# Expert results added up in DRAM by the scatters, in two sums that blocks use in turn

## The chip, the cores and the metric

The kernel runs on one core of a Trainium2 chip. The metric is the time of one execution on the device, in microseconds, lower is better; a kernel's time is the median over its runs. Engines are called as in the profile: PE (TensorE; PEld are its weight loads), DVE (VectorE), ACT (ScalarE), POOL (GpSimd), and SP, which here only issues DMAs. "SPq", "ACTq" and "POOLq" are their queues.

## What is computed

One decoder layer on x of 16 sequences of 256 tokens with 256 features (4096 tokens in all), in f32. Three steps, each followed by a sum with its input and a layer norm:

```python
x = layernorm(x + attention(x))                  # one head, its own weighting function before the softmax
x = layernorm(x + cross_attention(x, ctx, ctx))  # 16 heads, in chunks of 64 positions
x = layernorm(x + ffn(x))
# ffn: 32 experts of width 128, each token goes to 4 of them, plus one shared expert of width 256
mixed  = (sel * topk_w[:, :, None]).sum(1)       # sel: the 4 chosen experts' outputs of a token
shared = (silu(h @ sg.T) * (h @ su.T)) @ sd.T
ffn    = mixed + shared
```

The change concerns the last step: how the four expert results of a token, its shared part and its residual come together before the last layer norm.

## The kernel before

**Phase 1, one sequence after the other.** A software pipeline over t in range(nseq + 5) runs attention, cross attention, the router and the shared expert of several sequences at once. Each engine has its own hand-written order of steps, guarded by semaphores; the queue of SP is one such order: `load_xT`, `load_x`, `load_c`, `store_acc`, `load_rest`. `load_rest(i)` fills the DRAM table `routed` with zeros once (at i == 0) and loads a sixteenth of the expert weights for each i. `vec_acc` forms residual + shared expert for two tokens per partition and `store_acc` writes them to the DRAM tensor `base` (4096 rows of 1 KB). POOL scatters each token's row four times into `routed`, into the regions of its experts (`pool_scattera`, `pool_scatterb`), with the gate weight and the destination row in two more columns.

**Phase 2, blocks of 128 rows.** The rows of one expert form blocks; there are 160 blocks, handled in turns of 8 (`UNROLL`). For each block SP loads 128 rows into one of 16 buffers `rowsb` (L1494), PE transposes them (`pe_xbT`, L277), multiplies with the gate and up weights (`pe_gu`, L583), transposes the hidden block, multiplies with the down weights (`pe_down`, L596); ACT scales the result by the gate weight into one of four buffers `yb` (`act_yb`, L924) once the scatter of four blocks before has landed; DVE computes the destination rows `idcol` (`vec_idx`, L1246), where rows beyond a block's end go to rows that nobody reads; POOL scatters `yb` into the DRAM tensor `y` (L1419). `y` has a row of its own for each of the 4 choices of each token, 16384 rows, so no two scatters touch the same row and none waits for another. Behind the row load of block 16, SP issues one load of the whole of `base` into `base_sb` (L1497).

**Phase 3, the end.** SP waits until all scatters have landed. Then 16 groups (`GROUPS`) of two tokens per partition (`FT` = 2): SP loads the four rows of each token into one of 8 buffers `f4` (`STEPS`, L611), from group 8 on only once the store of eight groups before has landed. POOL adds rows 2 and 3 (L652) and `base_sb` (L655); DVE adds rows 0 and 1 (L620), then POOL's sum (L622), takes `bn_stats` and `bn_aggr` (L626, L629), adds epsilon (L631); POOL takes the power -0.5 (L661), one group late; DVE makes the bias (L636), ACT normalizes (L674) and stores (L678).

Of the kernel before, what the change touches and what calls it, by code (L numbers as in the profile page):

```python
# [5 lines left out]
P = 128  # L6
D = 256
DK = D // P
S = 256
T = S // P  # L10
# [13 lines left out]
ROWS = 16  # L24
YS = 4
FT = 2
STEPS = 8
# [6 lines left out]
    "a_tanh", "a_v", "a_vo", "a_x1", "a_x1T", "a_x2", "a_x2T", "a_xbT", "a_yb", "a_z", "g_frs", "g_iota", "g_own",  # L34
    "g_pow1", "g_pow2", "g_row", "g_rs1", "g_rs2", "g_sum", "g_xc", "g_xc2", "ld_base", "ld_cT", "ld_const", "ld_w",
    "ld_we", "ld_x", "ld_xT", "p_av1", "p_av2", "p_den", "p_down", "p_gu", "p_hbT", "p_k", "p_out2", "p_pTa",
    "p_pTb", "p_prT", "p_q", "p_rank", "p_router", "p_s1", "p_s2", "p_setup", "p_sg", "p_shout", "p_spread", "p_su",
    "p_tab", "p_v", "p_vo", "p_x1T", "p_x2T", "p_xbT", "p_z", "st_base", "st_rowa", "st_rowb", "st_zrow", "v_acc",
    "v_const", "v_fve", "v_h1", "v_hb", "v_hb1", "v_hbT", "v_hs", "v_idx", "v_idx1", "v_key", "v_msel", "v_mx",
    "v_mxa", "v_mxb", "v_nblk", "v_nmr", "v_o", "v_onehot", "v_own", "v_r", "v_rden", "v_rep", "v_route", "v_setup",  # L40
    "v_sha", "v_shb", "v_sum", "v_tab", "v_ve1", "v_ve2", "v_zrow",
# [12 lines left out]
def constants(nseq):  # L54
# [15 lines left out]
        n * TOPK + np.arange(blocks)[None, :] * P + p[:, None],  # L70
# [8 lines left out]
def build(nc, d, out):  # L79
# [9 lines left out]
    y = nc.dram_tensor("y", (TOPK * N + BLOCKS * P, D), F32).ap()  # L89
    base = nc.dram_tensor("base", (N, D), F32).ap()  # L90

    ctx = ExitStack()
    with ctx:
        def sb(name, shape, dt=F32):
            return ctx.enter_context(nc.sbuf_tensor(f"{name}_tile", shape, dt))
# [134 lines left out]
        base_sb = sb("base_sb", [P, TILES, D])  # L230
        f4 = [w_flat[:, u * TOPK * FT * D:(u + 1) * TOPK * FT * D].rearrange("p (k t d) -> p k t d", k=TOPK, t=FT)
# [370 lines left out]
        def flat(a):  # L602
            return a.rearrange("p t d -> p (t d)")

        def sync_out(e):
            for a in range(YS):
                e.wait_ge(SEM[f"st_y{a}"], 16 * BLOCKS // YS)
            for g in range(GROUPS):
                u = g % STEPS
                after(e, SEM[f"st_out{u}"], 16 * (g // STEPS))  # L610
                e.dma_start(f4[u][:, :, :, :],  # L611
                            y[0:TOPK * N, :].rearrange("(k p j) d -> p k j d", k=TOPK, p=P)
                            [:, :, g * FT:(g + 1) * FT, :]).then_inc(SEM[f"ld_f{u}"], 16)

        def vec_out(e, ch):

            def sums(g):
                u, n = g % STEPS, g // STEPS + 1
                e.wait_ge(SEM[f"ld_f{u}"], 16 * n)
                ch(e.tensor_tensor(flat(f4[u][:, 0, :, :]), flat(f4[u][:, 0, :, :]), flat(f4[u][:, 1, :, :]), ALU.add))  # L620
                e.wait_ge(SEM["g_sum"], g + 1)
                e.tensor_tensor(flat(f4[u][:, 0, :, :]), flat(f4[u][:, 0, :, :]), flat(f4[u][:, 2, :, :]), ALU.add)\  # L622
                    .then_inc(SEM["v_sum"], 1)
                e.wait_ge(SEM["v_sum"], g + 1)
                for t in range(FT):
                    m = e.bn_stats(fst[u][:, t, :], f4[u][:, 0, t, :])  # L626
                ch(m)
                for t in range(FT):
                    m = e.bn_aggr(fag[u][:, t, :], fst[u][:, t, :])  # L629
                ch(m)  # L630
                e.tensor_scalar(fve[u][:, :], fag[u][:, :, 1], LN_EPS, None, ALU.add).then_inc(SEM["v_fve"], 1)  # L631
# [13 lines left out]
        def pool_out(e):  # L645

            def sums(g):
                u, n = g % STEPS, g // STEPS + 1
                if g == 0:
                    e.wait_ge(SEM["ld_base"], 16)  # L650
                e.wait_ge(SEM[f"ld_f{u}"], 16 * n)
                e.tensor_tensor(flat(f4[u][:, 2, :, :]), flat(f4[u][:, 2, :, :]), flat(f4[u][:, 3, :, :]), ALU.add)\  # L652
                    .then_inc(SEM["g_own"], 1)
                e.wait_ge(SEM["g_own"], g + 1)
                e.tensor_tensor(flat(f4[u][:, 2, :, :]), flat(f4[u][:, 2, :, :]),  # L655
                                flat(base_sb[:, g * FT:(g + 1) * FT, :]), ALU.add).then_inc(SEM["g_sum"], 1)
# [740 lines left out]
        def _(e):  # L1397
            e.iota(dest_id[:, :, :], [[N, TOPK], [1, T]], base=-T, channel_multiplier=TILES).then_inc(SEM["g_iota"], 1)
            e.wait_ge(SEM["v_setup"], 1)
            e.wait_ge(SEM["v_const"], 1)  # L1400
            for t in range(nseq + 5):
# [12 lines left out]
                if live(t - 3):  # L1414
                    pool_row(e, t - 3)
            for n in range(BLOCKS):
                e.wait_ge(SEM["a_yb"], n + 1)
                e.wait_ge(SEM["v_idx"], n + 1)
                e.indirect_dma_start(y, bass.IndirectOffsetOnAxis(ap=idcol[n % ROWS][:, :], axis=0), yb[n % YS][:, :],  # L1419
                                     None).then_inc(SEM[f"st_y{n % YS}"], 16)  # L1420
# [4 lines left out]
        def _(e):  # L1425
# [32 lines left out]
            def load_rest(e, i):  # L1458

                if i == 0:  # L1460
# [4 lines left out]
                        .then_inc(SEM["st_zrow"], 16)  # L1465
                share = E // nseq * 3 * D
# [22 lines left out]
            for n in range(BLOCKS):  # L1489
# [5 lines left out]
                if n == ROWS:  # L1495
                    e.wait_ge(SEM["st_base"], 16 * nseq)
                    e.dma_start(base_sb[:, :, :], base.rearrange("(p j) d -> p j d", p=P)).then_inc(SEM["ld_base"], 16)  # L1497
# [51 lines left out]
```

## Time and profile before

| | us |
|---|---|
| median of 3 runs | 902.51 (901.99 to 903.1) |
| the profiled execution: its time | 904.18 |
| its span in the profile | 902.4 |
| first scatter to y / last scatter to y, start | 559.9 / 827.9 |
| first load of the end, start | 830.4 |

| engine | busy us | share of the span |
|---|---|---|
| PE | 761.9 | 84% |
| DVE | 581.8 | 64% |
| ACT | 464.1 | 51% |
| POOL | 451.5 | 50% |

The shares are averages over three phases with different limits: phase 1 ends at about 548 us, phase 2 at 830, phase 3 at 902. Within each, the windows and the timeline tell more than the page's totals. A POOL row for a scatter covers the issuing of the DMA, not its landing; the landing is a separate figure.

### The profile page before, as it was taken

What the parts mean: (1) busy time and instruction counts of PE and PEld (TensorE: products, weight loads), DVE (VectorE), ACT (ScalarE), POOL (GpSimd) and SP (SyncE); (2) the same over time, 40 slices, a digit from 0 to 9 for tenths busy, and PEclk for the clock granted to TensorE, in tenths of its full rate; (3) what the DMA queues carried; (4) which work ended last, traced back from release to release, by engine and by line L of the source; (5) the groups of instructions that cost most, each with busy time, mean ns of one, the idle gap of its engine ahead of it and who ended that gap; (6) DMA issues with size and microseconds to landing.
All of it is one profiled execution on the core that took longest, in us unless ns stands there. A gap on an engine that the chain in (4) does not pass through costs nothing.

```text
span 902.4 us, 24334 instructions
## 1 busy us (share of the span) xinstructions
PE 761.9 (84%) x7772; PEld 640.7 (71%) x7772; DVE 581.8 (64%) x2337; ACT 464.1 (51%) x1185; POOL 451.5 (50%) x533
## 2 busy tenths in 40 slices
PE   4678899999999999999999566899999999995000
PEld 3457788888888888888887444688888888884000
DVE  1233488888888788888888764454555545552897
ACT  0335665656656566566664102466666666663122
POOL 0011115545555454654645662455555555554997
PEclk9779999999999999999999866999999999998555
DMA  5083113323243232433331123955455555443994
GB/s 215 23 189 130 49 53 126 118 93 96 104 136 116 93 105 98 136 102 102 98 132 62 61 99 107 321 171 165 151 166 158 157 164 158 156 147 110 392 337 162
DMA packets 68909, 125.39 MB, mean 139 GB/s; under 512 B 9649, under 2 KB 42417, under 8 KB 68402
## 3 DMA queue, kind: packets, MB, share of 16 engines
q1 hardware_dynamic: 50610, 81.74, 29.8%
q0 software_dynamic: 13824, 37.90, 11.2%
q10 hardware_dynamic: 4352, 4.20, 1.3%
q8 instruction: 67, 1.10, 0.5%
q14 instruction: 56, 0.46, 0.2%
HBM read 73.30 MB, written 50.50 MB: 137 GB/s over the span
## 4 chain that ended last, share of the span: by engine, by line
PE 78%; DVE 10%; issue 3%; DMA 3%; POOL 2%; ACT 2%; SPq 0%; ACTq 0%; POOLq 0%; DVEq 0%
PE bank L583 14%; PE bank L277 11%; PE bank L596 7%; PE bank L392 4%; PE bank L353 3%; PE bank L313 3%; PE bank L540 3%; PE bank L380 3%; PE bank L334 3%; PE bank L370 3%; PE bank L325 3%; PE bank L486 3%; PE bank L528 3%; DVE w_expert_tile L620 3%; PE bank L517 3%
## 5 line engine op out<-in xcount | busy, mean ns | idle before, releaser
L1419 POOL DMA_INDIRECT y<-yb_tile,idcol_tile x160 | 153.4, 959 | 131.3 <-ACT yb_tile L924 129.0
L583 PE MATMUL bank<-w_expert_tile,xbT_tile 128*128 x640 | 168.8, 387 | 4.1 <-ACT xbT_tile L759 4.1
L1253 DVE COPY hbT_tile<-bank 128x128 f32<-128x128 f32 x160 | 46.6, 292 | 123.6 <-PE bank L277 123.6
L583 PEld LDWEIGHTS bank<-w_expert_tile,xbT_tile 128*128 128x128 f32 x640 | 110.4, 192 | 16.5 <-issue 7.8
L1386 POOL DMA_INDIRECT routed<-row_tile,idx_tile x64 | 63.0, 985 | 86.6 <-PE bank L409 67.1
L924 ACT ACTIVATE yb_tile<-bank,rowsb_tile 128x256 f32<-128x256 f32 x160 | 75.7, 473 | 47.9 <-PE bank L596 41.8
L596 PE MATMUL bank<-w_expert_tile,hbT_tile 128*128 x320 | 95.8, 381 | 0.0
L1354 POOL TENSOR_TENSOR rs_tile<-ve_tile,half_neg_tile 128x2 f32<-128x2 f32 x16 | 11.4, 715 | 157.2 <-DVE ve_tile L1023 157.2
L918 ACT ACTIVATE gb_tile<-bank 128x128 f32<-128x128 f32 x160 | 44.4, 278 | 61.7 <-PE bank L583 61.7
L1393 POOL DMA_INDIRECT routed<-row_tile,idx_tile x64 | 65.7, 1027 | 17.7 <-issue 17.7
L759 ACT ACTIVATE xbT_tile<-bank 128x256 f32<-128x256 f32 x160 | 60.1, 376 | 26.3 <-PE bank L277 25.9
L277 PE MATMUL bank<-const_tile,rowsb_tile 128*128 128x128 f32 x320 | 62.7, 278 | 2.7 <-DMA rowsb_tile<-routed 2.5
L277 PEld LDWEIGHTS bank<-const_tile,rowsb_tile 128*128 128x128 f32 x320 | 43.9, 143 | 23.2 <-issue 6.1
L596 PEld LDWEIGHTS bank<-w_expert_tile,hbT_tile 128*128 128x128 f32 x320 | 48.3, 191 | 12.6 <-issue 0.6
L1236 DVE SCALAR_TENSOR_TENSOR hb_tile<-gb_tile,bank 128x128 f32<-128x128 f32 x160 | 44.8, 280 | 8.9 <-ACT gb_tile L918 8.8
L1240 DVE TENSOR_TENSOR hb_tile<-hb_tile,bank 128x128 f32<-128x128 f32 x160 | 45.9, 287 | 5.6
L674 ACT ACTIVATE w_expert_tile<-w_expert_tile,fnmr_tile,frs_tile 128x256 f32<-128x256 f32 x32 | 17.5, 593 | 56.2 <-DVE fnmr_tile L636 55.7
L277 PE MATMUL bank<-const_tile,hb_tile 128*128 128x128 f32 x160 | 43.6, 273 | 0.0
L1370 POOL COPY row_tile<-x_tile 128x512 f32<-128x512 f32 x64 | 37.0, 619 | 5.3 <-DMA routed<-row_tile,idx_tile 5.3
L1348 POOL TENSOR_TENSOR xc_tile<-x_sb_tile,c_out_tile 128x256 f32<-128x256 f32 x32 | 23.0, 740 | 30.7 <-DVE c_out_tile L1286 26.9
L540 PE MATMUL bank<-w_shared_out_tile,hs_tile 128*128 128x256 f32 x128 | 34.7, 419 | 0.3 <-DVE hs_tile L1161 0.3
L313 PE MATMUL bank<-xT_tile,g_qk_tile 128*128 128x256 f32 x128 | 33.1, 405 | 2.2 <-DVE c_out_tile L1286 2.2
(206 smaller groups left out, 1863.1 us busy)
## 6 DMA issues: line engine op xcount, KB each, us to landing
rowsb_tile<-routed SPq DMA_DIRECT2D x160, 129.0 KB, 2.2
w_expert_tile<-y SPq DMA_DIRECT2D x16, 1024.0 KB, 8.8
w_expert_tile<-w_expert SPq DMA_DIRECT2D x16, 768.0 KB, 6.3
cT_tile<-ctxT SPq DMA_DIRECT2D x16, 384.0 KB, 3.5
routed<-zrow_tile SPq DMA_DIRECT2D x1, 4128.0 KB, 22.5
xT_tile<-xT SPq DMA_DIRECT2D x16, 256.0 KB, 3.3
x_sb_tile<-x SPq DMA_DIRECT2D x16, 256.0 KB, 3.6
base<-acc_sb_tile SPq DMA_DIRECT2D x16, 256.0 KB
```

What stands on the lines that cost most here:

```text
L277: return e.transpose(o, i, ident)
L313: m = e.matmul(bank[1][:, db * S:(db + 1) * S], g_qk[:, k, db * P:(db + 1) * P], xT[:, k, :], start=k == 0, stop=k == DK - 1)
L540: m = e.matmul(bank[0][:, t * D:(t + 1) * D], hs[:, k, t * P:(t + 1) * P], w_shared_out[:, k, :], start=k == 0, stop=k == DK - 1)
L583: m = e.matmul(bank[2 + u % 2][:, 0:2 * EI], xbT[u % 2][:, k * P:(k + 1) * P], w_flat[:, bass.ds(w * 3 * D + k * D, D)], start=k == 0, sto ...
L596: e.matmul(bank[6 + u % 2][:, 0:D], hbT[u % 2][:, :], w_flat[:, bass.ds(w * 3 * D + 2 * D, D)], start=True, stop=True).then_inc(SEM["p_dow ...
L759: e.activation(o, i, ACT.Copy).then_inc(SEM[done], 1)
L924: e.activation(yb[n % YS][:, :], bank[6 + u % 2][:, 0:D], ACT.Copy, scale=rowsb[n % ROWS][:, D:D + 1])\
L1240: e.tensor_tensor(hb[u % 2][:, :], hb1[u % 2][:, :], bank[2 + u % 2][:, EI:2 * EI], ALU.mult)\
L1253: e.tensor_copy(hbT[u % 2][:, :], bank[4 + u % 2][:, 0:EI]).then_inc(SEM["v_hbT"], 1)
L1386: e.indirect_dma_start(routed, bass.IndirectOffsetOnAxis(ap=idx[:, 0, k:k + 1], axis=0), row[:, k, 0, :], None).then_inc(SEM["st_rowa"], 16)
L1393: e.indirect_dma_start(routed, bass.IndirectOffsetOnAxis(ap=idx[:, 1, k:k + 1], axis=0), row[:, k, 1, :], None).then_inc(SEM["st_rowb"], 16)
L1419: e.indirect_dma_start(y, bass.IndirectOffsetOnAxis(ap=idcol[n % ROWS][:, :], axis=0), yb[n % YS][:, :], None).then_inc(SEM[f"st_y{n % YS} ...
```

## The change

The four rows per token in `y` give way to two sums, `y[0]` and `y[1]`, of one row per token each (plus 128 rows that nobody reads). The scatter of block n adds into `y[n % 2]` (`compute_op=ALU.add`). Since blocks of different experts can hold the same token, the scatter of block n waits until that of block n - 2 has landed. `base` is now the first 4096 rows of `y[0]`, so residual and shared part are in the sum from the start; `y[1]` and the unread rows of `y[0]` are filled with zeros by two stores that SP issues at i == 2 of phase 1. POOL waits for all base stores and both fills before its first scatter. The load of `base` is gone. The end loads two rows per token in place of four, has 16 buffers in place of 8, and adds the two rows: POOL for the second token of each partition, DVE for the first.

```diff
-STEPS = 8
+SUMS = 2
+STEPS = 16
...
-        n * TOPK + np.arange(blocks)[None, :] * P + p[:, None],
+        np.tile(n + p[:, None], (1, blocks)),
...
-    y = nc.dram_tensor("y", (TOPK * N + BLOCKS * P, D), F32).ap()
-    base = nc.dram_tensor("base", (N, D), F32).ap()
+    y = [nc.dram_tensor(f"y{u}", (N + P, D), F32).ap() for u in range(SUMS)]
+    base = y[0][0:N, :]
...
-        base_sb = sb("base_sb", [P, TILES, D])
...
-                e.dma_start(f4[u][:, :, :, :],
-                            y[0:TOPK * N, :].rearrange("(k p j) d -> p k j d", k=TOPK, p=P)
-                            [:, :, g * FT:(g + 1) * FT, :]).then_inc(SEM[f"ld_f{u}"], 16)
+                for k in range(SUMS):
+                    e.dma_start(f4[u][:, k, :, :],
+                                y[k][0:N, :].rearrange("(p j) d -> p j d", p=P)[:, g * FT:(g + 1) * FT, :])\
+                        .then_inc(SEM[f"ld_f{u}"], 16)
...
-                e.wait_ge(SEM[f"ld_f{u}"], 16 * n)
-                ch(e.tensor_tensor(flat(f4[u][:, 0, :, :]), flat(f4[u][:, 0, :, :]), flat(f4[u][:, 1, :, :]), ALU.add))
+                e.wait_ge(SEM[f"ld_f{u}"], 16 * SUMS * n)
+                ch(e.tensor_tensor(f4[u][:, 0, 0, :], f4[u][:, 0, 0, :], f4[u][:, 1, 0, :], ALU.add))
+                e.bn_stats(fst[u][:, 0, :], f4[u][:, 0, 0, :])
                 e.wait_ge(SEM["g_sum"], g + 1)
-                e.tensor_tensor(flat(f4[u][:, 0, :, :]), flat(f4[u][:, 0, :, :]), flat(f4[u][:, 2, :, :]), ALU.add)\
-                    .then_inc(SEM["v_sum"], 1)
-                e.wait_ge(SEM["v_sum"], g + 1)
-                for t in range(FT):
-                    m = e.bn_stats(fst[u][:, t, :], f4[u][:, 0, t, :])
-                ch(m)
+                ch(e.bn_stats(fst[u][:, 1, :], f4[u][:, 0, 1, :]))
...
-                if g == 0:
-                    e.wait_ge(SEM["ld_base"], 16)
-                e.wait_ge(SEM[f"ld_f{u}"], 16 * n)
-                e.tensor_tensor(flat(f4[u][:, 2, :, :]), flat(f4[u][:, 2, :, :]), flat(f4[u][:, 3, :, :]), ALU.add)\
-                    .then_inc(SEM["g_own"], 1)
-                e.wait_ge(SEM["g_own"], g + 1)
-                e.tensor_tensor(flat(f4[u][:, 2, :, :]), flat(f4[u][:, 2, :, :]),
-                                flat(base_sb[:, g * FT:(g + 1) * FT, :]), ALU.add).then_inc(SEM["g_sum"], 1)
+                e.wait_ge(SEM[f"ld_f{u}"], 16 * SUMS * n)
+                e.tensor_tensor(f4[u][:, 0, 1, :], f4[u][:, 0, 1, :], f4[u][:, 1, 1, :], ALU.add)\
+                    .then_inc(SEM["g_sum"], 1)
...
-            e.iota(dest_id[:, :, :], [[N, TOPK], [1, T]], base=-T, channel_multiplier=TILES).then_inc(SEM["g_iota"], 1)
+            e.iota(dest_id[:, :, :], [[0, TOPK], [1, T]], base=-T, channel_multiplier=TILES).then_inc(SEM["g_iota"], 1)
...
+            e.wait_ge(SEM["st_base"], 16 * nseq)
+            e.wait_ge(SEM["st_zero"], 16 * 2)
             for n in range(BLOCKS):
+                e.wait_ge(SEM["v_idx"], n + 1)
+                if n >= SUMS:
+                    e.wait_ge(SEM[f"st_y{(n - SUMS) % YS}"], 16 * ((n - SUMS) // YS + 1))
                 e.wait_ge(SEM["a_yb"], n + 1)
-                e.wait_ge(SEM["v_idx"], n + 1)
-                e.indirect_dma_start(y, bass.IndirectOffsetOnAxis(ap=idcol[n % ROWS][:, :], axis=0), yb[n % YS][:, :],
-                                     None).then_inc(SEM[f"st_y{n % YS}"], 16)
+                e.indirect_dma_start(y[n % SUMS], bass.IndirectOffsetOnAxis(ap=idcol[n % ROWS][:, :], axis=0),
+                                     yb[n % YS][:, :], None, compute_op=ALU.add).then_inc(SEM[f"st_y{n % YS}"], 16)
...
+                if i == 2:
+                    e.dma_start(y[1].rearrange("(j p) d -> p j d", p=P),
+                                zrow[:, 0:D].rearrange("p (j d) -> p j d", j=1).to_broadcast([P, N // P + 1, D]))\
+                        .then_inc(SEM["st_zero"], 16)
+                    e.dma_start(y[0][N:N + P, :], zrow[:, 0:D]).then_inc(SEM["st_zero"], 16)
...
-                if n == ROWS:
-                    e.wait_ge(SEM["st_base"], 16 * nseq)
-                    e.dma_start(base_sb[:, :, :], base.rearrange("(p j) d -> p j d", p=P)).then_inc(SEM["ld_base"], 16)
```

## Rows read from the trace of the kernel before

**Rows 1.** Windows: PE, PEld, DVE, ACT, POOL busy, clock, DMA share, GB/s

```profile
...
566.00:583.00 17.00, 12.93 (x69) 10.31 (x68) 6.17 (x29) 7.31 (x24) 6.92 (x8) 1.00 0.96 360
585.00:827.00 242.00, 240.33 (x1294) 196.41 (x1292) 121.52 (x578) 148.38 (x432) 139.53 (x147) 1.00 0.50 155
840.00:896.00 56.00, 0.00 (x0) 0.00 (x0) 53.90 (x121) 15.30 (x28) 54.13 (x45) 0.50 0.88 311
```

**Rows 2.** Timeline of POOL, expert stretch: start, length, instruction, idle before

```profile
...
559.90 0.96 POOL L1419 DMA_INDIRECT y<-yb_tile,idcol_tile  x1 [15.67 <-ACT yb_tile L924]
...
571.29 0.96 POOL L1419 DMA_INDIRECT y<-yb_tile,idcol_tile  x1 [0.67 <-ACT yb_tile L924]
...
585.86 0.96 POOL L1419 DMA_INDIRECT y<-yb_tile,idcol_tile  x1 [0.67 <-ACT yb_tile L924]
...
602.48 0.96 POOL L1419 DMA_INDIRECT y<-yb_tile,idcol_tile  x1 [0.67 <-ACT yb_tile L924]
604.40 0.96 POOL L1419 DMA_INDIRECT y<-yb_tile,idcol_tile  x1 [0.96 <-ACT yb_tile L924]
```

**Rows 3.** Timeline of the end, the first sum, one group, the last power

```profile
...
835.83 0.69 DVE L620 TENSOR_TENSOR w_expert_tile<-w_expert_tile 128x512 f32<-128x512 f32 x1 [11.30 <-DMA w_expert_tile<-y]
...
882.00 1.76 DVE L620 TENSOR_TENSOR w_expert_tile<-w_expert_tile 128x512 f32<-128x512 f32 x1
...
883.18 1.14 POOL L661 TENSOR_TENSOR frs_tile<-fve_tile,fhalf_tile 128x2 f32<-128x2 f32 x1
...
883.80 0.69 DVE L622 TENSOR_TENSOR w_expert_tile<-w_expert_tile 128x512 f32<-128x512 f32 x1
884.29 1.32 POOL L652 TENSOR_TENSOR w_expert_tile<-w_expert_tile 128x512 f32<-128x512 f32 x1
...
885.69 1.27 POOL L655 TENSOR_TENSOR w_expert_tile<-w_expert_tile,base_sb_tile 128x512 f32<-128x512 f32 x1
885.74 1.76 DVE L620 TENSOR_TENSOR w_expert_tile<-w_expert_tile 128x512 f32<-128x512 f32 x1
...
897.06 0.69 POOL L661 TENSOR_TENSOR frs_tile<-fve_tile,fhalf_tile 128x2 f32<-128x2 f32 x1 [1.52 <-DVE fve_tile L631]
```

**Rows 4.** Page, group of POOL's 128x256 sums: busy us, mean ns

```profile
...
L1348 POOL TENSOR_TENSOR xc_tile<-x_sb_tile,c_out_tile 128x256 f32<-128x256 f32 x32 | 23.0, 740 | 30.7 <-DVE c_out_tile L1286 26.9
```

**Rows 5.** Timeline, the last scatter and the first load of the end

```profile
...
827.92 0.96 POOL L1419 DMA_INDIRECT y<-yb_tile,idcol_tile  x1 [0.30 <-issue]
830.36 50.03 SPq L611 DMA_DIRECT2D w_expert_tile<-y  x16
```

**Rows 6.** DMA issues of the whole run: count, KB each, median us to landing

```profile
...
rowsb_tile<-routed SPq DMA_DIRECT2D x160, 129.0 KB, 2.2
...
routed<-zrow_tile SPq DMA_DIRECT2D x1, 4128.0 KB, 22.5
...
base_sb_tile<-base SPq DMA_DIRECT2D x1, 4096.0 KB, 13.9
```

**Rows 7.** Timeline of SP's queue around the two places of a fill

```profile
...
50.01 10.74 SPq L1467 DMA_DIRECT2D w_expert_tile<-w_expert  x1
...
109.70 1.40 SPq L1467 DMA_DIRECT2D w_expert_tile<-w_expert  x1
121.31 0.33 SPq L1438 DMA_DIRECT2D xT_tile<-xT  x1
```

**Rows 8.** DMA issues from 49 to 72 us, the load behind the fill

```profile
...
w_expert_tile<-w_expert SPq DMA_DIRECT2D x1, 768.0 KB, 23.9
```

**Rows 9.** Timeline of PE, first use of the xT in question

```profile
...
143.12 1.89 PE L313 MATMUL bank<-xT_tile,g_qk_tile 128*128 128x256 f32 x8
```

**Rows 10.** All scatters to y: us from issue to landing

```profile
...
DMA to landing us min/median/max: 2.4/2.5/11.0
```

**Rows 11.** DMA queues from 585 to 827 us: packets, MB, share of 16 engines

```profile
...
q1 hardware_dynamic: 19518, 17.90, 28.9%
q0 software_dynamic: 7018, 19.19, 20.3%
```

More of the change, by code:

```diff
@@ L33 @@
     "a_gb", "a_hg", "a_k", "a_norm", "a_num", "a_pTa", "a_pTb", "a_pr", "a_prT", "a_q", "a_sc", "a_sha", "a_shb",
[L34 to L38, printed above, removed]
+    "a_tanh", "a_v", "a_vo", "a_x1", "a_x1T", "a_x2", "a_x2T", "a_xbT", "a_yb", "a_z", "g_frs", "g_iota", "g_pow1",
+    "g_pow2", "g_row", "g_rs1", "g_rs2", "g_sum", "g_xc", "g_xc2", "ld_cT", "ld_const", "ld_w", "ld_we", "ld_x",
+    "ld_xT", "p_av1", "p_av2", "p_den", "p_down", "p_gu", "p_hbT", "p_k", "p_out2", "p_pTa", "p_pTb", "p_prT",
+    "p_q", "p_rank", "p_router", "p_s1", "p_s2", "p_setup", "p_sg", "p_shout", "p_spread", "p_su", "p_tab", "p_v",
+    "p_vo", "p_x1T", "p_x2T", "p_xbT", "p_z", "st_base", "st_rowa", "st_rowb", "st_zero", "st_zrow", "v_acc",
     "v_const", "v_fve", "v_h1", "v_hb", "v_hb1", "v_hbT", "v_hs", "v_idx", "v_idx1", "v_key", "v_msel", "v_mx",
     "v_mxa", "v_mxb", "v_nblk", "v_nmr", "v_o", "v_onehot", "v_own", "v_r", "v_rden", "v_rep", "v_route", "v_setup",
-    "v_sha", "v_shb", "v_sum", "v_tab", "v_ve1", "v_ve2", "v_zrow",
+    "v_sha", "v_shb", "v_tab", "v_ve1", "v_ve2", "v_zrow",
     *(f"{n}{u}" for n in ("ld_f", "st_out") for u in range(STEPS)),
@@ L228, in build @@
         yb = [sb(f"yb{u}", [P, D]) for u in range(YS)]
-        base_sb = sb("base_sb", [P, TILES, D])
-        f4 = [w_flat[:, u * TOPK * FT * D:(u + 1) * TOPK * FT * D].rearrange("p (k t d) -> p k t d", k=TOPK, t=FT)
+        f4 = [w_flat[:, u * SUMS * FT * D:(u + 1) * SUMS * FT * D].rearrange("p (k t d) -> p k t d", k=SUMS, t=FT)
               for u in range(STEPS)]
```

## The prediction

> **What bounds the kernel now.** I read the table of windows first, to split the run into what is different: the expert stretch from 560 to 828 us and the end from 830 to 902 us. In the expert stretch TensorE is busy for 240.33 of 242 us at a granted clock of 1.00, POOL for 139.53, and the DMA engines half of the time [rows 1]. So there TensorE sets the pace, and everything else has room. The timeline of POOL gives that pace: scatters start at 559.90 and 571.29 with seven steps between them, 1.627 us each, and one step in eight is 1.92 (602.48 to 604.40), the turn's own cost; a turn of eight blocks takes 7 x 1.627 + 1.92 = 13.3 us [rows 2]. POOL issues for 0.96 us and sleeps for 0.67 until ACT has written yb [rows 2].
>
> At the end TensorE does nothing. Between 840 and 896 POOL is busy for 54.13 of 56 us and DVE for 53.90 [rows 1]. The timeline of one group there (882.00 to 885.74, 3.74 us) shows POOL without a gap: L661 1.14, L652 1.32, L655 1.27, together 3.73 [rows 3]. DVE's L620 takes 1.76 where L622, the same shape, takes 0.69 [rows 3]: it sits beside POOL's operations, so DVE's full look is partly waiting. POOL's three operations bound the end, and the DMA engines, 0.88 busy at 311 GB/s [rows 1], are close behind.
>
> **The end, step by step.** Each of the 16 groups moves 1.05 MB in and 0.26 MB out now; after, 0.52 MB in and 0.26 out, 12.6 MB in all against 21. At full business the two DMA-heavy stretches give 311/0.88 = 353 and 360/0.96 = 375 GB/s [rows 1], so 12.6 MB take 33.5 to 35.6 us, 2.1 to 2.2 us per group. POOL keeps one sum of 128x256 (0.74 by L1348, the same kind and shape [rows 4]) and the power (0.69 alone, 1.14 beside DVE [rows 3]): 1.4 to 1.9 us. DVE loses L620 (1.76), has half of L622 (about 0.36, up to 0.9 if it is stretched in the ratio of L620 to L622), and keeps the statistics and small operations, 3.74 - 1.76 - 0.69 = 1.3: 1.7 to 2.2 us. Three engines near 2 us; the largest is the DMA, and I take 2.15. The sixteen buffers in place of eight take away the loads' wait for stores, so nothing else holds the loads back.
>
> The first sum started 5.5 us after the first load's issue (830.36 to 835.83 [rows 3, 5]); with half the bytes (0.52 MB less at 360 GB/s is 1.5 us) it starts after about 4. Then fifteen groups of 2.15, then the last group: 1.9 on DVE and, as now from the last power's start to the end of the span, 902.4 - 897.06 = 5.3 us [rows 3]. That is 830.4 + 4 + 32.2 + 7.2 = 873.8, against 902.4: 28.6 us saved. The bounds: with 1.8 us per group 34, with 2.5 us 23.
>
> **The base load.** base_sb, 4.1 MB with 13.9 us to landing [rows 6], is issued among the row loads and does collide: from 571.29 to 585.86 six steps take 14.57 us where 6 x 1.627 = 9.8 would do [rows 2], in the stretch where the DMA engines are 0.96 busy [rows 1]. It goes away whole: 4.8 us saved.
>
> **The zero fill.** A new store of 4.3 MB is put into SP's queue at i == 2, like the fill of routed at i == 0, which took 22.5 us to land [rows 6] and whose follower, a weight load at 50.01, held SP's issue for 10.74 us [rows 7] and landed after 23.9 [rows 8]. The new one comes at about 109.7; the weight load behind it then issues until about 121, when SP turns to the next xT anyway (121.31) [rows 7]. What is late is the xT and x of the next sequence. By the first fill the weight load is in 24 us after the fill's issue, here at 134, and xT and x, 0.26 MB each behind it, by about 136; TensorE wants xT at 143.12 [rows 9]. Seven microseconds of cover, so zero. Were the loads later than that, TensorE would wait once for what overruns 143.12: a fill of twice the length, 45 us, would cost 15. The second fill (0.13 MB) and POOL's waits for the last base store lie long before the first scatter at 559.90; both cost nothing. POOL's iota only changes its pattern.
>
> **The scatters: the unknown.** POOL must now see scatter n - 2 landed before it issues n, and each scatter also adds. Behind the wait on POOL stands every later scatter; ACT waits for them by the four yb buffers, then TensorE through the banks. So a pair of blocks costs at least L + r, L from issue to landing, r from the landing to the next issue. TensorE's own pace gives 13.3 / 4 = 3.33 us per pair. The plain scatter has L = 2.4 to 2.5 [rows 5, 10]. For r, POOL's gap between issues with nothing to wait for is 0.30 [rows 5], and I take 0.25. So the plain scatter would need 2.7 of 3.33: the turn-taking alone is free, and adding may cost L another 0.6 before it shows (L = 3.08). Beyond that each 0.1 us of L costs 80 pairs x 0.1 = 8 us. The gain of 33 us is gone at L = 3.5.
>
> No row shows an adding DMA. The lower bound is that of the plain one, 2.4. The upper bound, a read that is done before the write begins: a row load from DRAM, 2.2 us [rows 6], and then the scatter, 2.4, or 4.6. Between them: the scatters' queue takes 20.3% of 242 us on the DMA engines for 147 scatters, 0.33 us each [rows 11]. If each row is read as well, and rows are pipelined, that is another 0.33 us, and a DRAM access ahead of the first. A row load's engine time is 28.9% of 242 us over 134, 0.52 us [rows 11]; of its 2.2 us the other 1.7 are issue, access and landing, and I give the access 0.3, because SP's issue alone takes 0.33 at least [rows 7] and the landing is a way of its own. That makes L = 3.1. It is nearer to the pipelined end since a scatter's 128 rows are independent, eight for each engine. Then: 80 x 0.02 and some irregular landings, about 2 us, and 0.6 for the last landing. DMA engines then are some two thirds busy, not full. Were the issue on POOL longer too, it would bind by itself from 13.3 / 8 - 0.30 = 1.36 us; 0.96 now.
>
> What the rows show is a scatter whose 0.33 us of engine time is a small part of its 2.4 us [rows 10, 11]. The Trainium skill, page Collectives: The Full Stack, section on the bandwidth ceiling, says that a reduction in the DMA engine is slower because it needs two source reads, not for the addition. By that rule alone L would be about 2.8 and the stretch would stay free; my sum has 3.1.
>
> **The sum**, against the profiled execution's 904.2 us: -28.6 (end) - 4.8 (base) + 0 (fill) + 2.6 (scatters) = -31, so 873; that execution is 1.7 above the median of 902.5, so 872.
>
> **The rivals.** (1) The same mechanism, with an adding scatter of 3.2 to 3.45 us: part of the gain is paid back on the pairs, 880 to 899 us. For it: 0.1 to 0.4 us over my L is nothing beside a price that no row shows. Against: the engine time doubled explains only 0.33.
> (2) The other side: L above 3.5. POOL's wait for st_y of n - 2 replaces ACT's yb as what ends its idle time, TensorE starves, and the kernel is slower. At L = 4.0 a pair takes 4.25, 74 us more than 3.33 over 80 pairs, 943 us; at the bound of 4.6, 122 us more, 991 us. For it: landing is latency, not bytes, and an adding scatter has two latencies in a row. Against: pipelining. In that bound the read is 2.2 us; the Trainium skill, DMA: Bandwidth & Descriptors, section on latency, has 0.2 us on average and 2 us at high load for an HBM access, so by its second figure this rival would win; the trace has no row for it. The engines here are half busy [rows 1].
> (3) Making descriptors for an addition doubles POOL's issue: 1.92 + 0.30 = 2.22 per block against 1.66, 90 us more, some 959 us. Nothing in the rows speaks for a doubling; the routed scatters cost the same issue with other rows.
> (4) The end is held by something else (DVE and POOL taking turns on every group, 2.5 us per group): 878.
>
> **The numbers.** My forecast, L at most 3.2 with the end as worked out, has 0.46 and, alone, the range 864 to 881. Rival 4 has 0.05, rival 1 has 0.14. Rival 2 has 0.29 (0.16 of it up to 945), rival 3 has 0.04. About 0.02 is left where gain and loss cancel. So faster by over 0.2% 0.65, within 0.2% (1.8 us, about what a measurement of this kernel can tell from no change) 0.02, slower 0.33. The range for 8 in 10 goes from 864 to 945, leaving out the longest landings and the doubled issue.
>
> **What would show it.** Right: POOL's idle time before the scatters still ended by ACT's yb; scatters' landing below 3.1; steps of 1.63 without the hole at 571; TensorE busy over 0.95 in the stretch; the end about 43 us long with 2.1 to 2.2 us from group to group; the sequence after the fill no longer than the others. Wrong: POOL waiting for the y landings, granted clock and TensorE's share falling between 560 and 828, an issue above 1.36 us.

## The result: slower by 9.6%

The changed kernel takes 989.34 us (median of 4 runs, 986.5 to 989.91) where the kernel before takes 902.25 beside it. The ratio is 1.096, 95% interval 1.0935 to 1.0984. The forecast was 872 us, in a range of 864 to 945. The profiled execution took 986.5 us, its span is 984.7.

The windows give the same columns as [rows 1]: busy PE, PEld, DVE, ACT, POOL, clock, DMA share, GB/s.

```profile
585.00:827.00 242.00, 179.34 (x890) 137.45 (x888) 90.32 (x395) 91.45 (x294) 153.46 (x99) 0.99 0.66 108
...
950.00:980.00 30.00, 0.00 (x0) 0.00 (x0) 26.98 (x110) 15.89 (x30) 24.95 (x32) 0.50 1.00 366
```

TensorE is busy for 179 of 242 us in the expert stretch, against 240 [rows 1]; its granted clock is still at the upper level of 2.4 GHz (0.99), so the clock has no part in the loss. At the end the DMA engines are now full. POOL's timeline shows the stretch (the answer to [rows 2]):

```profile
588.83 1.56 POOL L1415 DMA_INDIRECT y<-yb_tile,idcol_tile  x1 [1.30 <-ACT yb_tile L916]
590.69 1.56 POOL L1415 DMA_INDIRECT y<-yb_tile,idcol_tile  x1 [0.30 <-issue]
593.80 1.56 POOL L1415 DMA_INDIRECT y<-yb_tile,idcol_tile  x1 [1.54 <-ACT yb_tile L916]
595.66 1.56 POOL L1415 DMA_INDIRECT y<-yb_tile,idcol_tile  x1 [0.30 <-issue]
598.69 1.56 POOL L1415 DMA_INDIRECT y<-yb_tile,idcol_tile  x1 [1.47 <-ACT yb_tile L916]
```

Two things are new. The issue takes 1.56 us in place of 0.96. And the scatters come in pairs, 4.97 and 4.89 us from pair to pair, where TensorE's pace is 3.33. The releaser in these rows misleads: ACT's yb named here is not the one that POOL scatters next. ACT's own row says what it starts on:

```profile
593.16 0.47 ACT L916 ACTIVATE yb_tile<-bank,rowsb_tile 128x256 f32<-128x256 f32 x1 [2.43 <-DMA y<-yb_tile,idcol_tile]
```

ACT waits for the landing of the scatter issued at 588.83, because its buffer of four comes free with it, and POOL's scatter of 593.80 waits for that same landing, because it adds into the same sum; its own yb had been written from 588.19 on. The trace's record of that landing has 593.08, 4.25 us after the issue. Both were asleep on this one event: ACT starts 0.08 us after it and POOL 0.72 us after it, and 4.25 + 0.72 is the pair's 4.97. POOL starts 0.64 us after ACT, and since ACT's write of 0.47 us has ended just before, the profile puts POOL's idle time down to ACT. The waits of ACT from 585 to 927 us (us in total, times, longest) and the chain of the page tell the cause plainly:

```profile
ACT yb_tile L916 <- DMA y<-yb_tile,idcol_tile: 196.3, 133, 3.6
```

```profile
PE 47%; DMA 41%; DVE 6%; issue 2%; ACT 2%; POOL 1%; SPq 1%; ACTq 0%; POOLq 0%; DVEq 0%
DMA y<-yb_tile,idcol_tile 39%; PE bank L277 5%; PE bank L392 3%; PE bank L353 3%; PE bank L380 3%; PE bank L313 3%; PE bank L540 3%; PE bank L334 3%; PE bank L370 3%; PE bank L325 3%; PE bank L486 3%; PE bank L528 2%; PE bank L517 2%; PE bank L409 2%; PE bank L463 2%
```

39% of the span is the landing of scatters; the chain before had 3% of DMA in all. The landing itself (answer to [rows 10]) and the queues from 585 to 927 us (answer to [rows 11]; packets, MB, share of the 16 engines):

```profile
DMA to landing us min/median/max: 3.7/3.9/5.5
```

```profile
q0 software_dynamic: 20092, 18.31, 44.6%
q1 hardware_dynamic: 19219, 17.63, 20.8%
```

141 scatters take 44.6% of 342 us, 1.08 us of every DMA engine for one, where it was 0.33. The bytes of one scatter are the same, 0.13 MB, in three times the packets: 20092 for 141 scatters against 7018 for 147. The packet records give the sizes: an adding scatter has 128 packets of 1024 bytes and 16 of 4, a plain one 32 of 4096 and 16 of 4. A packet takes 0.12 us on average here and 0.11 before, so the larger number of packets is nearly the whole increase.

The end, in its timeline (answer to [rows 3] and [rows 5]):

```profile
942.03 1.56 POOL L1415 DMA_INDIRECT y<-yb_tile,idcol_tile  x1 [0.83 <-issue]
945.90 17.34 SPq L612 DMA_DIRECT2D w_expert_tile<-y  x30
949.54 0.42 DVE L621 TENSOR_TENSOR w_expert_tile<-w_expert_tile 128x256 f32<-128x256 f32 x1 [19.61 <-DMA w_expert_tile<-y]
...
957.84 0.41 DVE L621 TENSOR_TENSOR w_expert_tile<-w_expert_tile 128x256 f32<-128x256 f32 x1
957.93 0.88 POOL L653 TENSOR_TENSOR frs_tile<-fve_tile,fhalf_tile 128x2 f32<-128x2 f32 x1
...
958.78 0.72 POOL L647 TENSOR_TENSOR w_expert_tile<-w_expert_tile 128x256 f32<-128x256 f32 x1
...
959.51 0.41 DVE L621 TENSOR_TENSOR w_expert_tile<-w_expert_tile 128x256 f32<-128x256 f32 x1
```

From group to group it takes 1.67 us here, with POOL (0.88 + 0.72) and DVE both full; later it waits for loads. From the first load to the end of the span it is 984.7 - 945.9 = 38.8 us, where it was 72.0.

**Where the time went.** First scatter to last: 942.03 - 554.52 = 387.5 us against 268.0, +119.5 (the base load's hole is gone within it). The last scatter's landing: 3.9 against 2.4, +1.4. The end: -33.2. The first scatter comes 5.4 us earlier, in an execution whose granted clock rose sooner near the start (0.91 and 0.88 against 0.77 and 0.81 from 10 to 30 and from 30 to 50 us). That is not the change's: of the thirteen traces of this document, the four with 0.91 there (this one, plain_turns, norows_add, add_filler) have the first scatter at 554 to 555 us, the nine others at 556.6 to 564.8. Together 119.5 + 1.4 - 33.2 - 5.4 = 82.3, which is 984.7 - 902.4.

### The profile page after: what moved, and what is told of

Read it like the earlier page. It is cut to its first block, busy times and chain, and to the rows that moved or that the text cites. A ratio compares the mean times of both kernels' runs of the same rounds, so it can differ in the third digit from the quotient of the medians.

```text
span 984.7 us, 24307 instructions
## 1 busy us (share of the span) xinstructions
PE 778.1 (79%) x7772; PEld 639.2 (65%) x7772; DVE 564.4 (57%) x2321; ACT 451.0 (46%) x1185; POOL 515.0 (52%) x517
## 3 DMA queue, kind: packets, MB, share of 16 engines
HBM read 60.71 MB, written 54.95 MB: 117 GB/s over the span
## 4 chain that ended last, share of the span: by engine, by line
PE 47%; DMA 41%; DVE 6%; issue 2%; ACT 2%; POOL 1%; SPq 1%; ACTq 0%; POOLq 0%; DVEq 0%
DMA y<-yb_tile,idcol_tile 39%; PE bank L277 5%; PE bank L392 3%; PE bank L353 3%; PE bank L380 3%; PE bank L313 3%; PE bank L540 3%; PE bank L334 3%; PE bank L370 3%; PE bank L325 3%; PE bank L486 3%; PE bank L528 2%; PE bank L517 2%; PE bank L409 2%; PE bank L463 2%
## 5 line engine op out<-in xcount | busy, mean ns | idle before, releaser
L1415 POOL DMA_INDIRECT y<-yb_tile,idcol_tile x160 | 249.5, 1560 | 155.2 <-ACT yb_tile L916 110.1
L583 PE MATMUL bank<-w_expert_tile,xbT_tile 128*128 x640 | 177.2, 400 | 89.1 <-ACT xbT_tile L751 89.0
L910 ACT ACTIVATE gb_tile<-bank 128x128 f32<-128x128 f32 x160 | 44.6, 279 | 10.2 <-PE bank L583 9.2
L1340 POOL TENSOR_TENSOR xc_tile<-x_sb_tile,c_out_tile 128x256 f32<-128x256 f32 x32 | 23.0, 740 | 27.2 <-DVE c_out_tile L1278 23.5
L392 PE MATMUL bank<-x1T_tile,w_cross_tile 128*128 128x256 f32 x128 | 33.3, 405 | 0.7 <-ACT x1T_tile L751 0.7
## 6 DMA issues: line engine op xcount, KB each, us to landing
y<-zrow_tile SPq DMA_DIRECT2D x1, 4224.0 KB, 15.2
```

Source lines behind the costliest of these rows:

```text
L392: m = e.matmul(bank[0][:, db * S:(db + 1) * S], w_cross[:, k, 0, db * P:(db + 1) * P], x1T[:, k, :], start=k == 0, stop=k == DK - 1)
L583: m = e.matmul(bank[2 + u % 2][:, 0:2 * EI], xbT[u % 2][:, k * P:(k + 1) * P], w_flat[:, bass.ds(w * 3 * D + k * D, D)], start=k == 0, sto ...
L1415: e.indirect_dma_start(y[n % SUMS], bass.IndirectOffsetOnAxis(ap=idcol[n % ROWS][:, :], axis=0), yb[n % YS][:, :], None, compute_op=ALU.ad ...
```

## The experiments

Eleven kernels gave a result, in three groups, each beside the kernel before, whose medians there were 902.77 us (plain_turns, sums4, base_spread), 908.58 (yb8b, sums1 and the two fillers) and 904.14 (the two without row loads, wait_last, sums3). The medians of different groups are therefore compared by their ratios. A landing is the time from the start of POOL's issue to the last semaphore event of its DMA; in some traces it is on record for a part of the scatters only (120 of 160 in the changed kernel, 40 in plain_turns). Diffs are against the changed kernel unless stated.

### The turns without the addition (plain_turns)

```diff
-                                     yb[n % YS][:, :], None, compute_op=ALU.add).then_inc(SEM[f"st_y{n % YS}"], 16)
+                                     yb[n % YS][:, :], None).then_inc(SEM[f"st_y{n % YS}"], 16)
```

> The changed kernel with one edit: the scatters write and do not add (the later one wins, so the sums are not formed); the turns of two, the fills, the waits and the short end stay. My theory: the adding itself costs everything, through a longer issue on POOL (1.56 us in place of 0.96) and a later landing (3.9 in place of 2.5). With both back at the old values a pair needs about 2.5 + 0.7 = 3.2 us, under TensorE's 3.33, so the expert stretch takes about 263 us again and the kernel the 868 to 872 us of the prediction. Rival: the waiting in turns costs by itself, because POOL starts some 0.7 us (and more) after a landing; then a pair takes 3.6 or more and the kernel is at 890 or above.

The sums are not formed in this kernel, so only its time counts. 903.61 us, ratio 1.0008 (0.998 to 1.0035). The issue is back at 0.96 and the median landing at 2.5, yet the gain of the end is not there: first to last scatter takes 860.7 - 553.9 = 306.8 us. POOL's timeline shows two rhythms side by side:

```profile
598.53 0.96 POOL L1415 DMA_INDIRECT y<-yb_tile,idcol_tile  x1 [1.80 <-ACT yb_tile L916]
599.79 0.96 POOL L1415 DMA_INDIRECT y<-yb_tile,idcol_tile  x1 [0.30 <-issue]
602.55 0.96 POOL L1415 DMA_INDIRECT y<-yb_tile,idcol_tile  x1 [1.81 <-ACT yb_tile L916]
...
610.55 0.96 POOL L1415 DMA_INDIRECT y<-yb_tile,idcol_tile  x1 [1.80 <-ACT yb_tile L916]
612.17 0.95 POOL L1415 DMA_INDIRECT y<-yb_tile,idcol_tile  x1 [0.66 <-ACT yb_tile L916]
613.65 0.96 POOL L1415 DMA_INDIRECT y<-yb_tile,idcol_tile  x1 [0.53 <-ACT yb_tile L916]
615.27 0.96 POOL L1415 DMA_INDIRECT y<-yb_tile,idcol_tile  x1 [0.66 <-ACT yb_tile L916]
```

In step, 1.6 us apart, the turns cost nothing, as forecast. Bunched, a pair takes 4.02. The trace's DMA records say where that time is: the scatter issued at 610.55 has its 48 packets from 612.09 to 612.57, 1.54 us after the issue. Those of the pair of 598.53 and 599.79 lie together, 96 packets from 600.84 to 601.95, so none comes sooner than 2.31 us after the first issue, and a row load lies beside them, at 600.08 to 601.14. So "the turn-taking alone is free" was wrong: the turns turn a delayed landing, which nobody used to wait for, into a delay of everything.

### The same without row loads (norows_plain, norows_add)

From block 16 on, the load of 128 rows becomes a load of one row into a buffer that nobody reads, and the destination rows are p * 32 + n mod 32. norows_plain also has plain scatters. The blocks work on the rows of the first sixteen over and over, so only the times count.

```diff
...
-                e.dma_start(rowsb[n % ROWS][:, :], routed[bass.ds(at, P), :]).then_inc(SEM[f"ld_row{n % ROWS}"], 16)
+                if n < ROWS:
+                    e.dma_start(rowsb[n % ROWS][:, :], routed[bass.ds(at, P), :]).then_inc(SEM[f"ld_row{n % ROWS}"], 16)
+                else:
+                    e.dma_start(dummy[n % ROWS][:, :], routed[bass.ds(at, 1), :]).then_inc(SEM[f"ld_row{n % ROWS}"], 16)
```

> As plain_turns (scatters in turns of two that write and do not add), and from block 16 on the row load of 129 KB is replaced by one of a single row into a buffer that nobody reads; the blocks work on the rows of the first sixteen, and their destination rows are p * 32 + n mod 32. So everything is there but the row loads' traffic. In sums1 a lone adding scatter shows L = 3.8 and a step of 4.46, so r = 0.66; for a plain one that makes 2.5 + 0.66 = 3.16 us per pair, under TensorE's 3.33. My theory: the 4.0 us of a bunched pair in plain_turns are row loads that come onto the DMA engines together with the scatters; without them the pair keeps up with TensorE, the stretch takes about 262 us and the kernel 865 to 872 us. Rival: two scatters in flight hold up each other, or POOL does, whatever else runs: 895 us or more.

> The changed kernel with the same edit (no row traffic from block 16 on), adding scatters. My theory: a pair costs L + r of a lone scatter, 4.46, in place of 4.93, 38 us less: 948 to 955 us. If two adding scatters in flight also hold up each other (each has 1.1 us of every DMA engine) it stays between 4.46 and 4.93. Rival: 4.93 as before, 989 us.

norows_plain: 872.94 us, ratio 0.9657 (0.9601 to 0.9713), the scatters within 828.6 - 557.3 = 271.3 us. norows_add: 962.72, ratio 1.0686 (1.062 to 1.0752), 364.6 us. Their windows from 600 to 800 us, in this order:

```profile
600.00:800.00 200.00, 196.10 (x1053) 160.01 (x1052) 98.27 (x468) 118.11 (x352) 111.05 (x116) 1.00 0.22 78
```

```profile
600.00:800.00 200.00, 165.43 (x789) 121.88 (x789) 81.14 (x352) 80.53 (x264) 136.54 (x88) 1.00 0.50 59
```

With no row loads in the way TensorE is busy for 196 of 200 us under plain turns: the collision with the row loads is what ate plain_turns' gain, 306.8 - 271.3 = 35 us of the stretch. Adding scatters stay slow with the engines half idle; there the row loads are only 387.5 - 364.6 = 23 us of the loss. The rest is the adding scatter itself, under the turns. One thing besides the row loads differs: the destination rows are a regular pattern here. It did not make the scatters lighter (from 600 to 800 us a plain one takes 0.37 us of every engine, 0.33 in plain_turns, an adding one 1.13 against 1.08), but no run has the pattern alone.

### One sum (sums1)

Every scatter waits for the one before it, so the step measures landing plus wake-up alone. The fill of the second sum, the second load of the end and its addition are gone.

```diff
-SUMS = 2
+SUMS = 1
...
```

> One sum in place of two: every adding scatter waits for the landing of the one just before it, so that a scatter is alone and its step from start to start is L + r with nothing else of its kind in flight; the end loads one row per token and adds nothing. My theory: L is 3.9 and POOL starts about 0.6 us after the landing, a step of 4.5 us, 720 us for 160 blocks, an end of 30 to 35 us: 1300 to 1315 us in all. If the steps are 4.5, the 4.93 us per pair of the changed kernel hold 0.4 us of two scatters and their row loads in each other's way. Rival: the 4.93 are L + r alone (POOL wakes 1.0 us after a landing), a step of 4.9 us, about 1375 us.

1317.56 us (2 runs), ratio 1.4516 (1.4396 to 1.4635). The view of POOL's scatters gives the landing, and its timeline the step:

```profile
DMA to landing us min/median/max: 3.6/3.8/4.4
```

```profile
601.24 1.56 POOL L1412 DMA_INDIRECT y<-yb_tile,idcol_tile  x1 [2.98 <-ACT yb_tile L913]
605.70 1.55 POOL L1412 DMA_INDIRECT y<-yb_tile,idcol_tile  x1 [2.90 <-ACT yb_tile L913]
610.16 1.56 POOL L1412 DMA_INDIRECT y<-yb_tile,idcol_tile  x1 [2.90 <-ACT yb_tile L913]
```

The step is 4.46; over all 159 steps the mean is 4.52. The landing of the scatter of 601.24 is on record at 604.98, 3.74 after its issue, so r = 4.46 - 3.74 = 0.72 us. It is the same 0.72 in 150 of this kernel's 159 waits, and in the changed kernel, where 118 landings can be compared, no scatter starts sooner than 0.72 after the one that it needs. ACT, asleep on the same landing, starts at 605.07, 0.08 after it.

The packet records also divide L. The adding scatter of 601.24 has its packets from 603.37 to 604.65 and is landed at 604.98. In the kernel before, the plain one of 606.03 has them from 607.56 to 608.06 and is landed at 608.42. From the issue to the first packet it is 2.13 us against 1.53, the packets take 1.28 against 0.50, and from there to the landing it is 0.33 against 0.36. So of the 1.35 us by which L grew here, 0.60 lies ahead of the first packet, exactly as much as POOL's issue grew, and 0.78 is the longer run of packets. The row load beside this step (601.66 to 602.49) is over before the packets begin. Reads of the destination rows show nowhere: the page has 60.71 MB read from HBM for the changed kernel and for plain_turns alike.

### Is r the order of the waits? (wait_last)

```diff
+                e.wait_ge(SEM["a_yb"], n + 1)
                 if n >= SUMS:
                     e.wait_ge(SEM[f"st_y{(n - SUMS) % YS}"], 16 * ((n - SUMS) // YS + 1))
-                e.wait_ge(SEM["a_yb"], n + 1)
```

> The changed kernel with POOL's wait for the landing of scatter n - 2 put last, behind that for yb, in place of before it. POOL starts 0.66 us after a landing, ACT at once. My theory: part of the 0.66 is the instructions that POOL still has between the wait and the issue; with the wait directly ahead of the issue 0.2 to 0.3 us less per pair, 965 to 975 us. Rival: the 0.66 is POOL's own start of an indirect DMA after it slept, whatever the order: 989 us.

992.18 us, ratio 1.0979 (1.0909 to 1.1048), pairs of 4.88 (600.90 to 605.78) and 4.81. The theory fell: r does not come from a wait that POOL has yet to look at behind the landing. By the landing records it is 0.76 us here, not less than 0.72.

### Is it the buffers? (yb8b)

Eight `yb` buffers in place of four, with eight `f4` buffers so that the semaphores suffice. With sixteen of them (yb8) they don't, and that kernel has no time.

```diff
-YS = 4
+YS = 8
...
-STEPS = 16
+STEPS = 8
```

> The changed kernel with eight yb buffers in place of four, and eight buffers at the end in place of sixteen (for the number of semaphores). My theory: ACT and POOL wait for the same landing, ACT because it is two blocks ahead and out of buffers, POOL because of the turn of two; more yb buffers give nothing in the expert stretch (388 us), and the end is at most a few us longer: 986 to 994 us. Rival: the four buffers are the bound, so that eight give back much of the loss, down to POOL's own 1.86 us per block, about 895 us.

991.16 us, ratio 1.0922 (1.0826 to 1.1018), pairs of 5.00 and 4.62 (602.46, 607.46, 612.08). ACT's 196 us of waiting were a follower's: given more buffers, it changes nothing, because POOL's own wait sets the pace. The profile still puts 108.7 us of POOL's idle time down to ACT's yb, although with eight buffers a block's yb is written some 15 us before its scatter: that releaser can't be the one waited for.

### Breaking the bunches (plain_filler, add_filler)

A memset of a buffer that nobody reads, behind each scatter on POOL, meant to keep a pair apart. plain_filler has plain scatters.

```diff
...
+                after(e, SEM["g_fill"], n - 3)
+                e.memset(filler[n % YS][:, :], 0.0).then_inc(SEM["g_fill"], 1)
```

> As plain_turns (scatters that write and do not add, in turns of two), with one more POOL operation behind each scatter, a memset of 128x256 of a buffer that nobody reads, some 0.3 us. In plain_turns the scatters go in two ways: in step with TensorE, 1.55 to 1.62 us apart and landing in 2.5, or bunched, two of them 1.26 us apart and 4.02 us per pair, where both are held up by the row loads that are released with them. My theory: bunching, not turn-taking as such, costs the 31 us between 903 and 872; the filler keeps two scatters apart, the bunches are left, and the kernel comes to 870 to 885 us. Rival: POOL's late waking sets the 4 us per pair; then the filler changes nothing or adds, 903 us or more.

> The changed kernel with the same filler behind each adding scatter. POOL then needs 1.56 + 0.3 + 0.3 + some gap, about 2.3 us per block. My theory: the pair is no longer bunched and costs 4.5 to 4.6 us in place of 4.93, 30 us less, 955 to 965 us, although POOL has more to do. Rival: a pair is L + r whatever lies between, 987 us; or, if POOL's own chain counted, slower than 989.

906.4 us, ratio 0.9977 (0.9936 to 1.0018), and 989.64, ratio 1.0924 (1.0839 to 1.1009). Both expectations of a gain were wrong. The plain scatters stay bunched, at 600.91, 602.37 and 604.99, 606.45: the first pair takes 4.08 and the next two 3.88 and 3.94, though the scatters are now 1.46 apart within one. In add_filler the scatters are 2.07 and 3.21 apart (599.64, 601.71, 604.92), so the memset does spread them, but a pair still takes 4.6 to 5.3 us. Spreading the two scatters within a pair does not shorten it.

### More sums (sums4, sums3)

Scatter n waits for n - 4 or n - 3, far longer ago. The price is more loads and sums at the end.

```diff
-SUMS = 2
-STEPS = 16
+SUMS = 4
+STEPS = 8
...
```

> Four sums in turn, with three big zero fills at i = 2 to 4, eight buffers at the end, four rows loaded per token, no base load: POOL adds two of them, DVE the other two and both sums. A scatter now waits for the one four blocks before, as ACT's yb does anyway. My theory: the chain of landings binds with two sums (4.93 us per pair); with four it allows (3.9 + 0.7) / 4 = 1.2 us per block, and then POOL's issue binds, 1.56 + 0.30 = 1.86 us per block: 298 us for the stretch in place of 388, and an end of about 68 us, 920 to 930 us in all. Rival: the DMA engines' own work on adding scatters (1.1 us each on every engine, beside 0.5 for the row load) or a landing that gets later with more of them in flight keeps the block at 2.2 us or more: 970 us or above.

> Three sums in turn, two big zero fills, sixteen buffers at the end, three rows loaded per token (POOL adds two of them, DVE the third). Chain: (3.9 + 0.66 and up to 0.5 for bunching) / 3 = 1.5 to 1.7 us per block; POOL's issue 1.86: 298 us for the stretch. End: 0.79 MB in and 0.26 out per group, 2.9 us, 54 us in all. My theory: 554 to 560 + 298 + 4 + 54, 910 to 916 us, a ratio of 1.01: between two sums (the chain binds) and four (issue binds, long end), and still no faster than before. Rival: with three the landing chain still binds with growing landings, 940 us or above.

sums4 takes 923.53 us, ratio 1.0219 (1.0187 to 1.0251); sums3, which keeps STEPS = 16, takes 917.86, ratio 1.0155 (1.0102 to 1.0207). POOL in sums3 runs without a pause:

```profile
602.12 1.56 POOL L1416 DMA_INDIRECT y<-yb_tile,idcol_tile  x1 [0.30 <-DMA y<-yb_tile,idcol_tile]
603.98 1.56 POOL L1416 DMA_INDIRECT y<-yb_tile,idcol_tile  x1 [0.30 <-DMA y<-yb_tile,idcol_tile]
```

Each scatter follows 0.30 us behind the one before, the gap with nothing to wait for; a wait for a landing would have cost 0.72. So hardly any landing is waited for, although the profile names one, and the step is 1.86 against TensorE's 1.66: POOL's issue is the bound now. The scatters take 862.3 - 560.4 = 301.9 us, 159 x 1.86 = 296 and some irregular ones. Freed of the chain, adding is still slower than before: 34 us lost in the stretch, about 19 won at the end (its 52.7 us against 72.0).

### The part of the change that is a gain (base_spread)

The kernel before, with its load of `base` cut into 16 pieces, one behind every eighth row load:

```diff
...
-                if n == ROWS:
-                    e.wait_ge(SEM["st_base"], 16 * nseq)
-                    e.dma_start(base_sb[:, :, :], base.rearrange("(p j) d -> p j d", p=P)).then_inc(SEM["ld_base"], 16)
+                if n >= ROWS and n % UNROLL == 0 and n // UNROLL - 2 < 16:
+                    g = n // UNROLL - 2
+                    if g == 0:
+                        e.wait_ge(SEM["st_base"], 16 * nseq)
+                    e.dma_start(base_sb[:, g * FT:(g + 1) * FT, :],
+                                base.rearrange("(p j) d -> p j d", p=P)[:, g * FT:(g + 1) * FT, :])\
+                        .then_inc(SEM["ld_base"], 16)
```

> The kernel before with one edit: the load of base_sb is cut in 16 pieces of 256 KB, one behind every eighth row load from block 16 on, in place of one of 4 MB behind block 16. Theory: the hole of 4.8 us at 571 us comes from that one load and goes away, ratio about 0.995, 897 to 898 us. Rival: the same bytes cost the same wherever they lie (each piece delays the row loads or scatters near it a little), 902 us.

895.84 us (6 runs), ratio 0.993 (0.9906 to 0.9955). The window of the hole has a full TensorE (17.00 of 17 us against 12.93), at a DMA share of 0.70 in place of 0.96 [rows 1]:

```profile
566.00:583.00 17.00, 17.00 (x93) 13.75 (x91) 8.80 (x44) 10.49 (x31) 9.84 (x11) 1.00 0.70 210
```

Of the versions that form the whole result this is the only one below the kernel before, by 0.7%, a small gain whose interval leaves out 1. From first to last scatter it takes 822.4 - 558.8 = 263.6 us against 268.0, so the base load's collision was worth 4.4 us by the trace (4.8 forecast), and it needs no addition in DRAM to be avoided. Of the 6.9 us between the medians, the other 2.5 are not explained by it.

## Why the prediction was wrong, step by step

- **The step that failed is the term for the scatters: +2.6 us by the forecast, 0.6 of them for the last landing; +119.5 and +1.4 measured, and 4.4 more if one counts the hole that went away inside it.** Its form was right, a pair costs at least L + r, but every size in it was off in one direction:
  - *L*, issue to landing: 3.1 taken, 3.9 measured, within the bounds of 2.4 and 4.6. I chose near the lower end by the argument that rows are pipelined over the engines and that an addition only doubles 0.33 us of engine time. It went up to 1.08, with packets of 1 KB in place of 4 KB. And I had kept the issue out of L: the first packet comes after it, so its 0.60 us more are in every landing.
  - *r*, landing to next issue: 0.25 taken, 0.72 measured (sums1). I took it from POOL's gap between issues with nothing to wait for, which is no wake-up.
  - *The issue on POOL*: called unchanged, 1.56 measured. Two of them with their gaps are 3.72 us: more than TensorE's 3.33, so past the point of 1.36 that I had named, but less than the 4.87 of a pair, so not what sets the pace here. It does set that of sums3 and sums4.
  - *What passes in between*: nothing was counted for row loads meeting scatters. 23 us here (norows_add), 35 us on plain scatters. It sits in the landing of a pair's first scatter: 4.25 us for that of 588.83, whose first packet comes only 2.85 us after the issue, with a row load at 590.88 to 592.05.

  In a pair: 387.5 us over 79.5 pairs is 4.87. 3.74 + 0.72 = 4.46 is the usual step of the lone chain (sums1), 4.52 its mean, 364.6 / 79.5 = 4.59 with two in flight and no row loads, and 0.28 more with them. Against 3.33 that is some 1.5 us for each of 80 pairs.
- **The sentence "the turn-taking alone is free" failed too.** It holds only where nothing disturbs a landing (nearly so in norows_plain, and in the stretches in step of plain_turns). With r at 0.72 a plain pair needs 2.5 + 0.72 = 3.2 of TensorE's 3.33, so there was a margin of 0.1 us where I saw 0.6.
- **Rival 2, with 0.29, is what happened**, by its place (POOL behind the landing of n - 2, ACT behind the buffers, TensorE starved) and by its price (943 to 991 for L from 4.0 to 4.6). That its price fits is partly luck: with the measured L of 3.9 its own sum gives some 935 us, and r and the row loads, which it did not count, stand for the rest.
- **The signs**: "POOL's idle time still ended by ACT's yb" was to show that I was right, and the profile does name ACT's yb, though POOL waits for landings. The granted clock, whose fall was a sign of being wrong, stayed at 0.99. The shares of TensorE and the issue above 1.36 us did tell.
- **Rival 3** (a longer issue) was right that it grows, by 0.6 us and not 0.96. That nothing in the rows spoke for it was no evidence against: no row had an adding DMA.
- **The two-reads rule** (the Trainium skill, Collectives: The Full Stack, bandwidth ceiling) points the right way and is too mild here: two reads for one would give about twice the engine time, the rows show 1.08 / 0.33 = 3.3 times. Whether there are two reads stays open, since no trace here counts the second; what is on record is the threefold number of packets. The 2 us that the Trainium skill (DMA: Bandwidth & Descriptors, latency) allows an HBM access at high load, by which rival 2 would win, is not needed to explain a landing longer by 1.3 to 1.4 us: the issue and the packets account for it.
- **The end: right in mechanism, better than forecast by 4.6 us** (33.2 saved, 28.6 forecast). Of a group DVE needs 1.67 us (1.7 to 2.2 forecast) and POOL 1.6 (1.4 to 1.9), and 366 GB/s was reached where I had 353 to 375. From group to group it is 1.82 on average (POOL's first sum at 949.59, its sixteenth at 976.87) where I took 2.15: the loads run ahead from 945.9 on, and 12.6 MB at 366 GB/s are 34.4 us from there, while my sum let sixteen groups of full transfer begin after the first load. The fourth of rivals, the two taking turns, did not appear.
- **The base load: right**, as base_spread shows by itself. Of the 4.8 us, 0.3 were a misreading: one of the six steps, the one after 571.29, is the long one of a turn (1.92), which leaves 4.5 where 4.4 was measured.
- **The fill: right, at zero.** It landed in 15.2 us where I went by 22.5, and TensorE's step from one sequence to the next over it, at L392, takes 105.02 to 131.91 = 26.9 us; at the same place before it was 110.64 to 137.84, 27.2.

What stays open: what POOL does in the 0.6 us by which it starts behind ACT, and what makes a bunch of plain scatters hold for several pairs and then let go. That it goes away without the row loads is shown (with the regular rows as a reservation); the filler did not part them.

## What to carry to other kernels

Work that nobody waits for has a latency that costs nothing; once something waits for it, the whole of it counts, with the wake-up of the engine and every collision on the way. Before a DMA is put into a dependent chain, size the chain by a row of a waiter that really was asleep on a landing, not by a gap between issues, and where the operation has no row, run the lone chain first. An estimate that lies right on the pace it must keep (3.35 against 3.33 us here) forecasts nothing. When the profile names a releaser that could not have been the one waited for, look for a third event on which both were asleep.

## What the runs showed of the hardware

- A scatter of 128 rows of 1 KB that adds (`ALU.add`, f32, into DRAM) costs 1.56 us of POOL's issue against 0.96, lands after 3.8 to 3.9 us against 2.5, and takes 1.08 us of every DMA engine against 0.33. It has 128 packets of 1 KB where the plain one has 32 of 4 KB, each packet taking 0.11 to 0.13 us in both.
- POOL starts an adding scatter 0.72 us after a landing on which it sleeps (sums1, and the changed kernel), where ACT, asleep on the same one, starts 0.08 us after it.
- The fill of 4.2 MB with rows of 1024 bytes landed in 15.2 us; the one of 4.1 MB with rows of 1032 bytes takes 22.5 [rows 6] and 23.0 in this kernel.
- Plain scatters under turns keep either of two rhythms for several pairs, 1.6 us apart or bunched at about 4.0 a pair.
